# First loop of a two-layer transformer kernel: queries and keys projected once, their split parts placed by on-chip transfers

## The chip, the cores and the metric

The kernel runs on one core of a Trainium2 chip. The metric is the device time of one execution of the whole program in microseconds (us). The core has five engines that run their own instruction streams and wait for one another through semaphores: PE (TensorE, matmuls), DVE (VectorE), ACT (ScalarE), POOL (GpSimd) and SP (SyncE, which here only issues transfers, or DMAs).

## The reference, cut to what matters

The program is a layer of four blocks, twice over. The change touches the first block alone, whose attention part is this, for B = 16 batches of N = 256 rows of D = 128 numbers, in H = 16 heads of Dh = 8:

```python
q = (x @ Wq).reshape(B, N, H, Dh)
k = (x @ Wk).reshape(B, N, H, Dh)
scores = jnp.einsum('bqhd,bkhd->bhqk', q, k) * Dh ** (-0.5)
attn = jax.nn.softmax(scores, axis=-1)
std_out = jnp.einsum('bhqk,bkhd->bqhd', attn, v).reshape(B, N, D)
```

The same block has a second path (distances to 64 "splats", a small feed-forward net over them, a gate), an output projection and a layer norm. The two largest and smallest twentieths of the weights of a later feed-forward block are found by a search over the bits of a threshold, which runs beside the first loop: 32 rounds, each with a candidate threshold, a comparison of all weights with it, a count, and a decision.

## The kernel before, in words

`build` runs `loop_1`, `loop_2` and `phase_3` one after the other; only `loop_1` is touched. It takes the 16 batches as 128 pair steps, eight for a batch, each for one pair of heads. The list `stages` (L434 to L444) places every other piece of work at an offset in steps from its batch's first pair step, and each engine runs its own part of the list in the list's order (`run_in_order`, L213). So at pair step g the engine does `pair_step(g)`, then all stages that are due. In this text "odd 4" is pair step 4 of an odd-numbered batch, "even 0" pair step 0 of an even one.

**The heads' rows.** The scores need float32 accuracy from a matmul that reads rounded numbers (float32r). Each head has 32 partitions: three blocks of eight rows with the query (or key) in split form, then two rows for the row maximum, which are 1 on the key's side. With q = qh + ql and k = kh + kl (rounded part and rest) the three blocks multiply qh·kh, qh·kl and ql·kh. Four heads lie in the 128 partitions of one group, so `qT` and `kT` have four groups. To get this layout the weights are padded and repeated three times (`wq_pad`, `wk_pad`, L846 to L851), so that a batch needs four projections of two groups each: q0, k0, q1, k1 at offsets -8, -6, -4, -2 (`project_qk`, L475). ACT rounds each of them (`round_qk`, L740), DVE subtracts, by a per-partition factor 0 or -1 (`split_qk`, L905), and so writes the part that belongs to each row.

**The pair step.** PE computes the scores of a pair (L629) into the one buffer `ps_scores`, DVE takes the row maxima (L1021) and frees it. Eleven steps later (LAG) PE computes the same scores transposed with the maximum subtracted (L638) into the one buffer `ps_scoresT`, ACT takes the exponential (L812). On odd steps PE multiplies with the values (L651), and ACT reads the result (L820). The maxima of a batch go through DVE, PE (`turn_rows`, L585), ACT (L799) and four transfers of SP (`place_rows`, L1106) into two rows of each head of `qT`; PE waits for them at step 3 of the next batch.

**The four banks.** Everything else that PE writes goes through four PSUM banks. `PlannedRing.open` (L107) picks the bank whose planned release is the earliest and lets PE wait until it has been read.

**The search.** DVE makes a candidate (L950) in steps 1 and 5, after its decision on the round before; POOL compares the weights with it (four instructions, L1061); PE counts (`count`, L574) in step 4 and in step 0 of the next batch; DVE decides (L958 to L964) one step later. Each of these waits for the one before.

**SP's queue.** In order, in a batch's cycle: `place_rows` (offset 8, so step 0), `store` (offset 33, step 1), `load` of x and the context (offset -11, step 5, with the weight loads of the first three batches). SP runs ahead until a wait stops it. PE turns the loaded x (`project_x`, L472) in step 6, two batches ahead.

Of the kernel before, what the change touches and what calls it, by code (L numbers as in the profile page):

```python
# [28 lines left out]
P = 128  # L29
# [217 lines left out]
def loop_1(nc, A, K, x_mid):  # L247
    U = 16
    with ExitStack() as ctx:
        def sb(name, shape, dt=F32):  # L250
            return ctx.enter_context(nc.sbuf_tensor(name, shape, dt))
# [10 lines left out]
        wq = sb("wq_pad", [P, GROUPS, 4, 32])  # L262
        wk = sb("wk_pad", [P, GROUPS, 4, 32])
# [55 lines left out]
        rounded = two("qk_rounded", [P, 2 * N], F32R)  # L319
        qT = sets(3, "qT", [P, GROUPS, N], F32R)  # L320
        kT = sets(3, "kT", [P, GROUPS, N], F32R)
# [40 lines left out]
        wq_ready = sem("query_weights_ready")  # L362
        wk_ready = sem("key_weights_ready")
# [22 lines left out]
        rounded_ready = Counted(sem("rounded_ready"))  # L386
# [40 lines left out]
        for n in sizes:  # L427
# [4 lines left out]
        PIECE = NS // 2 // 4  # L432

# [3 lines left out]
            (-11, "load"), (33, "store"), (-8, "q0"), (-6, "k0"), (-4, "q1"), (-2, "k1"), (5, "gather"),  # L437
# [5 lines left out]
            (-8, "split_q0"), (-6, "split_k0"), (-4, "split_q1"), (-2, "split_k1"), (8, "turn_rows"),  # L443
# [5 lines left out]
        def _(pe):  # L449
# [25 lines left out]
            def project_qk(u, name, w, half):  # L475
                if name == "q" and half == 0:
                    ring.wait_read(pe, "xT", u)
                if u == 0 and half == 0:
                    pe.wait_ge(wq_ready if name == "q" else wk_ready, 1)
                ps = ring.open(pe, name, u, half, held=0.95)  # L480
                for g in range(2):
                    mm = pe.matmul(ps[:, g * N:(g + 1) * N], w[:, 2 * half + g, :, :].rearrange("p j d -> p (j d)"),
                                   xT[u][:], start=True, stop=True)
                mm.then_inc(ring.filled(name, u, half), 1)
# [141 lines left out]
            def scores(n, i, t):  # L626
                u, p = divmod(n, PAIRS)
                q, j = p // 2, 32 * (2 * (p % 2) + i)
                mm = pe.matmul(s_ps[:, i, t, :], qT[u][j:j + 3 * DH0, q, t * P:(t + 1) * P], kT[u][j:j + 3 * DH0, q, :],  # L629
                               start=True, stop=True)  # L630
                if t == NT - 1:
                    mm.then_inc(scores_full.sem, 1)

            def scores_T(n, i, kt):
# [3 lines left out]
                mm = pe.matmul(t_ps[:, i, kt, :], kT[u][j:j + rows_read, q, kt * P:(kt + 1) * P],  # L638
                               qT[u][j:j + rows_read, q, :], start=True, stop=True)
# [16 lines left out]
            def pair_step(g):  # L656
# [33 lines left out]
            steps = dict(project_x=project_x, q0=lambda u: project_qk(u, "q", wq, 0), k0=lambda u: project_qk(u, "k", wk, 0),  # L690
                         q1=lambda u: project_qk(u, "q", wq, 1), k1=lambda u: project_qk(u, "k", wk, 1), vg=project_vg,
# [11 lines left out]
        def _(act):  # L703
# [34 lines left out]
            order = [("q", 0), ("k", 0), ("q", 1), ("k", 1)]  # L738

            def round_qk(u, i):  # L740
                name, half = order[i]
                n = 4 * u + i
                if n == 1:
                    act.wait_ge(split_ready, 1)
                ps = ring.wait(act, name, u, half)
                if n >= 2:
                    before = order[(n - 2) % 4]
                    ring.wait_read(act, before[0], (n - 2) // 4, before[1])
                if name == "q":
                    act.activation(rounded[n][:], ps[:], ACT.Copy).then_inc(rounded_ready.sem, 1)  # L750
                else:
                    act.activation(rounded[n][:], ps[:], ACT.Identity, bias=pad_ones[:]).then_inc(rounded_ready.sem, 1)
# [69 lines left out]
            steps = dict(project_x=project_x, q0=lambda u: round_qk(u, 0), k0=lambda u: round_qk(u, 1),  # L822
                         q1=lambda u: round_qk(u, 2), k1=lambda u: round_qk(u, 3), vg=read_vg, influence0=influence0,
# [7 lines left out]
        def _(dve):  # L831
            setup = Chain(dve, dve_setup)
            setup.add(dve.memset(wk[:], 0.0))
            setup.add(dve.memset(wq[:], 0.0))
# [10 lines left out]
            for i in range(3):  # L845
                ins = dve.tensor_scalar(wq[:, :, :, DH0 * i:DH0 * (i + 1)], wq_raw[:].rearrange(heads, g=GROUPS, j=4),  # L846
                                        DH0 ** -0.5, None, ALU.mult)
            ins.then_inc(wq_ready, 1)
            for i in range(3):
                ins = dve.tensor_copy(wk[:, :, :, DH0 * i:DH0 * (i + 1)], wk_raw[:].rearrange(heads, g=GROUPS, j=4))  # L850
            ins.then_inc(wk_ready, 1)  # L851
# [51 lines left out]
            order = [("q", qT, 0), ("k", kT, 0), ("q", qT, 1), ("k", kT, 1)]  # L903

            def split_qk(u, i):  # L905
                name, dst, half = order[i]
                ps = ring.bank(name, u, half)
# [131 lines left out]
        def _(pool):  # L1039
# [5 lines left out]
            for i in range(3):  # L1045
                setup.add(pool.memset(v[i][:], 0.0))
# [2313 lines left out]
```

## Time and profile before

| | us |
|---|---|
| median of three runs | 1932.77 (1927.73 to 1934.17) |
| span of the profiled execution | 1930.1 |
| first loop within it | 0 to about 479 |
| PE busy in the whole span | 1723.1 (89%) |
| DVE, ACT, POOL busy | 1374.7, 1189.4, 1037.7 |

The profiled execution is 2.7 us below the median, inside the spread of the three runs. Busy shares are over all three phases; the chain that ended last, in the page's fourth part, lies in the last phase and says nothing of the first loop. For a change in the first loop one has to read that loop's own stretches and its order of time.

### The profile page before, as it was taken

The numbers are of one execution on the slowest core, as the hardware profiler recorded it, in microseconds if no ns is written. First come the engines' busy times: TensorE is split into PE (matmuls) and PEld (weight loads), VectorE is DVE, ScalarE is ACT, GpSimd is POOL, SyncE is SP. The second block draws the span as 40 slices with busy tenths as digits, with TensorE's granted clock in tenths as the row PEclk, the third lists the DMA queues.
The fourth block names the chain that finished last, engine by engine and source line by source line (L and its number), as shares of the span: only waits on it lengthen the run. The fifth ranks groups of instructions, "written<-read, shape, count | busy, mean of one in ns | idle before, by whom it ended". The sixth has DMA issues, their size and how long they took to land. (4 is left out here: it accounts for less than half of the span.)

```text
span 1930.1 us, 43925 instructions
## 1 busy us (share of the span) xinstructions
PE 1723.1 (89%) x15676; PEld 1312.7 (68%) x15676; DVE 1374.7 (71%) x4606; ACT 1189.4 (62%) x2858; POOL 1037.7 (54%) x1590
## 2 busy tenths in 40 slices
PE   7999999988899999999999999999879999589930
PEld 5666666656777777777777777776656667479930
DVE  6788888873767788888888888897657876611127
ACT  3566666642688777778778777776315776244412
POOL 3566676663245565655666565666421442175375
PEclk8999999999999999999999999999988999689975
DMA  2000000000200000000000000000000000345322
GB/s 56 9 13 15 15 16 15 12 5 27 75 1 2 1 2 7 8 7 8 7 8 7 6 3 7 6 4 6 6 27 15 27 21 16 99 70 75 60 64 83
DMA packets 57824, 44.03 MB, mean 23 GB/s; under 512 B 13952, under 2 KB 50186, under 8 KB 57482
## 3 DMA queue, kind: packets, MB, share of 16 engines
q1 hardware_dynamic: 52330, 30.11, 5.4%
q0 software_dynamic: 4608, 9.45, 3.3%
q8 instruction: 129, 2.11, 0.4%
q10 hardware_dynamic: 672, 1.67, 0.2%
q14 instruction: 85, 0.70, 0.1%
HBM read 26.52 MB, written 13.63 MB: 21 GB/s over the span
## 5 line engine op out<-in xcount | busy, mean ns | idle before, releaser
L2281 POOL TENSOR_SCALAR probs<-probs,rsums 128x128 f32<-128x128 f32 (+1 forms) x512 | 208.7, 426 | 307.6 <-DVE rsums L2178 306.7
L1061 POOL TENSOR_SCALAR at_least<-magnitudes,candidates 128x512 bf16<-128x512 f32 x128 | 198.2, 1564 | 151.3 <-DVE candidates L950 151.3
L2162 DVE CUSTOM_DVE_ANT_0 probs<-dist,pq,nmin 128x128 f32<-128x128 f32 (+1 forms) x512 | 181.2, 409 | 76.0 <-PE pq L1622 75.6
L1902 ACT ACTIVATE probs<-probs,low 128x130 f32<-128x130 f32 (+1 forms) x512 | 227.7, 460 | 6.3 <-DVE low L2162 6.2
L1021 DVE TENSOR_REDUCE negmax<-ps_scores 128x4 f32<-128x1024 f32 x128 | 156.2, 1221 | 53.6 <-PE ps_scores L629 51.9
L812 ACT ACTIVATE pT<-ps_scoresT 128x1024 f32<-128x1024 f32 x128 | 131.1, 1024 | 61.8 <-PE ps_scoresT L638 55.2
L2172 DVE COPY pT<-pq 128x384 f32<-128x384 f32 x256 | 129.8, 547 | 4.1 <-PE pq L1637 4.1
L1815 ACT ACTIVATE qn<-pq 128x512 f32<-128x512 f32 x128 | 77.2, 603 | 81.4 <-PE pq L1479 79.8
L1622 PE MATMUL pq<-k1T,q1T 64*128 64x128 f32 (+1 forms) x1024 | 119.3, 351 | 0.4 <-ACT k1T L1830 0.3
L3302 POOL DMA_INDIRECT m_x<-token_rows,m_idx_put x80 | 75.8, 947 | 80.7 <-DVE m_idx_put L3232 33.3
L3254 DVE COPY m_y<-pm 128x256 f32<-128x256 f32 x40 | 17.0, 424 | 140.6 <-PE pm L3140 140.6
L2087 DVE TENSOR_REDUCE ss<-sq 128x8 f32<-128x512 f32 x128 | 84.3, 675 | 30.9 <-ACT sq L1818 29.9
L1902 ACT ACTIVATION_READ_ACCUMULATOR probs<-probs,low 128x1 f32 x512 | 104.3, 204 | 0.0
L2898 DVE TENSOR_REDUCE cnegmax<-pc_scores 128x8 f32<-128x1024 f32 x64 | 78.2, 1222 | 25.8 <-PE pc_scores L2568 25.7
L1637 PE MATMUL pq<-ident,probs 128*128 128x128 f32 x512 | 91.4, 274 | 0.0
L2935 POOL TENSOR_SCALAR crstd<-cmv 128x4 f32<-128x4 f32 x16 | 3.7, 233 | 158.0 <-DVE cmv L2809 158.0
L2760 ACT ACTIVATE cpT<-pc_scoresT 128x1024 f32<-128x1024 f32 x64 | 65.5, 1024 | 33.7 <-PE pc_scoresT L2577 33.6
L1657 PE MATMUL pr_heads<-pT,v 128*64 128x256 f32 x512 | 83.5, 405 | 0.0
L1622 PEld LDWEIGHTS pq<-k1T,q1T 64*128 64x128 f32 x1024 | 67.5, 187 | 23.1 <-issue 22.2
L1671 PE MATMUL pr_out<-wo,o1T 128*128 128x128 f32 x512 | 77.9, 275 | 3.7 <-DVE l_r L2019 3.7
L1634 PE MATMUL pq<-ident,probs 128*128 128x128 f32 x256 | 77.3, 302 | 3.5 <-POOL probs L2281 3.4
L3140 PEld LDWEIGHTS pm<-m_w,m_hid 128*128 128x128 f32 x640 | 77.6, 192 | 2.0
(543 smaller groups left out, 5293.4 us busy)
## 6 DMA issues: line engine op xcount, KB each, us to landing
expert_answers<-m_y SPq DMA_DIRECT2D x40, 128.0 KB, 2.0
m_w<-in_L_ffn_moe_w_dram SPq DMA_DIRECT2D x16, 256.0 KB, 5.9
x<-in_x_dram SPq DMA_DIRECT2D x16, 128.0 KB, 2.2
x_mid<-x SPq DMA_DIRECT2D x16, 128.0 KB, 1.8
y<-x_mid SPq DMA_DIRECT2D x16, 128.0 KB, 2.2
x_mid<-y SPq DMA_DIRECT2D x16, 128.0 KB, 1.8
cx<-x_mid SPq DMA_DIRECT2D x8, 256.0 KB, 3.0
token_rows<-c_hn SPq DMA_DIRECT2D x8, 256.0 KB, 2.0
```

The costliest lines, as they stand in the source:

```text
L812: act.activation(pT[:, n % NPT].rearrange("p i k n -> p (i k n)"), t_ps[:].rearrange("p i k n -> p (i k n)"), ACT.Exp).then_inc(pT_ready.s ...
L1021: dve.tensor_reduce(negmax[u][:, :, j:j + 2, q].rearrange("p t j -> p j t"), s_ps[:], AX.X, ALU.max, negate=True).then_inc(negmax_ready.se ...
L1061: pool.tensor_scalar(at_least[:, a, :], mags[:, 512 * (a // 2):512 * (a // 2) + 512], cf[:, a:a + 1], None, ALU.is_ge).then_inc(mask_ready ...
L1622: mm = pe.matmul(ps[i][:, t * P:t * P + w], q1T[u][64 * i:64 * i + 64, p, t * P:(t + 1) * P], k1T[u][64 * i:64 * i + 64, p, 0:w], start=Tr ...
L1637: mm = pe.transpose(ps[:, (kt + 1) * P:(kt + 2) * P], probs[:, a + 1, first_key + kt * P:first_key + (kt + 1) * P], ident[:])
L1657: pe.matmul(tgt[:, 0:N], v1[u][:, 0, h * DH1:(h + 1) * DH1], pT[:, b, 0:2].rearrange("k t q -> k (t q)"), start=True, stop=False, skip_gro ...
L1902: ins = act.activation(probs[:, a, keys_nulls(i, w)], probs[:, a, keys_nulls(i, w)], ACT.Exp, bias=low[:, a, i:i + 1], scale=-1.0, accum_o ...
L2087: dve.tensor_reduce(ss[:, a, t, 8 * j:8 * j + 8], sq[:, j, :].rearrange("p (h d) -> p h d", d=DH1), AX.X, ALU.add).then_inc(ss_ready.sem, 1)
L2162: ins = dve.tensor_tensor_reduce(probs[:, a + t, keys(i, w)], dist[:, (1 - t) * P:N], ps[:, t * P:t * P + w], slopes[h], nmin[u][:, t, h:h ...
L2172: dve.tensor_copy(pT[:, (2 * m + i) % 4].rearrange("k t q -> k (t q)"), ps[:, 0:3 * P])\
L2281: ins = pool.tensor_scalar(probs[:, a + t, keys(i, w)], probs[:, a + t, keys(i, w)], rsums[:, a + t, i:i + 1], 1.0, ALU.mult, ALU.mult)
L2898: dve.tensor_reduce(negmax[u][:, :, j:j + 2, q].rearrange("p t j -> p j t"), s_ps[:], AX.X, ALU.max, negate=True).then_inc(negmax_ready.se ...
```

## The change

Queries and keys are projected once, without padding: the weight columns are reordered so that partition 32·j + 4·d + g holds number d of the head in place j of group g. One stage `qk` at offset -9 takes the place of q0, k0, q1, k1: two 256-column matmuls for a batch in place of eight. ACT rounds both into `parts` blocks 0 and 3 (one instruction in place of four), DVE writes the rests into blocks 1 and 2 (one in place of four) and signals after a wait. SP then places them: `place_qk` at offset -6 issues twelve DMAs a batch, each from 32 partitions of `parts` (two blocks of 256 numbers, 64 KB in all) into the eight rows of one part of one head place, in all four groups, of a joined `qkT`. The buffer has three sets as before, so from the fourth batch on the transfers wait until the last transposed scores of three batches earlier have been read. The ones on the key's side are written once by POOL at the start. Two clears of the padded weights on DVE go.

```diff
-            (-11, "load"), (33, "store"), (-8, "q0"), (-6, "k0"), (-4, "q1"), (-2, "k1"), (5, "gather"),
+            (-11, "load"), (33, "store"), (-9, "qk"), (5, "gather"),
...
-            (-8, "split_q0"), (-6, "split_k0"), (-4, "split_q1"), (-2, "split_k1"), (8, "turn_rows"),
+            (-9, "rest_qk"), (8, "turn_rows"), (-6, "place_qk"),
...
+            def project_qk(u):
+                ring.wait_read(pe, "xT", u)
+                if u == 0:
+                    pe.wait_ge(wqk_ready, 1)
+                ps = ring.open(pe, "qk", u, held=0.95)
+                for i, w in enumerate((wq, wk)):
+                    mm = pe.matmul(ps[:, i * N:(i + 1) * N], w[:].rearrange("p j d g -> p (j d g)"), xT[u][:],
+                                   start=True, stop=True)
+                mm.then_inc(ring.filled("qk", u), 1)
...
-                    if p % 4 == 0:
-                        ring.wait_read(pe, "k", u, p // 4)
+                    if p == 0:
+                        pe.wait_ge(*qk_placed[u % 2].at(PLACED * (u // 2 + 1)))
...
+            def round_qk(u):
+                ps = ring.wait(act, "qk", u)
+                if u >= 2:
+                    act.wait_ge(*qk_placed[u % 2].at(PLACED * (u // 2)))
+                act.activation(parts[u][:, 0:4:3, :], ps[:].rearrange("p (i n) -> p i n", i=2), ACT.Copy)\
+                    .then_inc(rounded_ready.sem, 1)
...
-            setup.add(dve.memset(wk[:], 0.0))
-            setup.add(dve.memset(wq[:], 0.0))
...
+            def rest_qk(u):
+                ps = ring.bank("qk", u)
+                dve.wait_ge(*rounded_ready.at(u + 1))
+                dve.tensor_tensor(parts[u][:, 1:3, :], ps[:].rearrange("p (i n) -> p i n", i=2),
+                                  parts[u][:, 0:4:3, :].bitcast(F32), ALU.subtract).then_inc(rest_ready.sem, 1)
+                dve.wait_ge(*rest_ready.at(u + 1))
+                dve.sem_inc(ring.read("qk", u), 1)
...
+            for i in range(3):
+                ins = pool.memset(qkT[i][:, :, 1, :].bitcast(F32), 1.0)
+            ins.then_inc(pool_keys, 1)
...
+                def place_qk(u):
+                    if u == 0:
+                        sp_eng.wait_ge(pool_keys, 1)
+                    sp_eng.wait_ge(*rest_ready.at(u + 1))
+                    if u >= 3:
+                        sp_eng.wait_ge(*pT_ready.at(PAIRS * (u - 2)))
+                    for j in range(4):
+                        for part, blocks in enumerate((slice(0, 4, 3), slice(0, 3, 2), slice(1, 4, 2))):
+                            rows_to = slice(32 * j + DH0 * part, 32 * j + DH0 * (part + 1))
+                            sp_eng.dma_start(qkT[u][rows_to].bitcast(F32),
+                                             parts[u][32 * j:32 * j + 32, blocks, :].bitcast(F32))\
+                                .then_inc(qk_placed[u % 2].sem, 16)
```

## Rows read from the trace of the kernel before

**Rows 1.** Windows, 50 us of the loop: us; busy (instructions) of PE, PEld, DVE, ACT, POOL; clock; DMA; GB/s

```profile
200.00:250.00 50.00, 46.89 (x584) 32.75 (x582) 42.04 (x107) 31.68 (x62) 33.75 (x31) 1.00 0.05 15
```

**Rows 2.** Groups by line, 150 to 350 us: line engine op out<-in shapes xcount | busy, mean ns | idle

```profile
L482 PE MATMUL ps<-xT,wk_pad 128*128 128x256 f32 x64 | 18.1, 405 | 0.0
L750 ACT ACTIVATE qk_rounded<-ps 128x512 fp32r<-128x512 f32 x16 | 9.6, 597 | 0.0
L909 DVE SCALAR_TENSOR_TENSOR qT<-qk_rounded,split_rows,ps 128x512 fp32r<-128x512 f32 x16 | 11.9, 742 | 1.4 <-DVE mixedT L999 1.3
```

**Rows 3.** Timeline of PE, one odd and one even batch: start us, us, engine line [idle before]

```profile
202.43 0.64 PE L585 MATMUL ps<-ident_r,max_rows 128*8 128x128 f32 x8 [1.09 <-DVEq L1002]
203.00 0.39 PE L629 MATMUL ps_scores<-kT,qT 24*128 24x256 f32 x2
207.85 0.39 PE L629 MATMUL ps_scores<-kT,qT 24*128 24x256 f32 x2 [0.76 <-DMA qT<-max_rowsT]
212.64 1.11 PE L574 MATMUL ps<-at_least,ones_bf 128*128 128x64 bf16 x32
213.69 0.38 PE L629 MATMUL ps_scores<-kT,qT 24*128 24x256 f32 x2
216.61 0.39 PE L629 MATMUL ps_scores<-kT,qT 24*128 24x256 f32 x2
218.53 0.39 PE L629 MATMUL ps_scores<-kT,qT 24*128 24x256 f32 x2
219.80 0.46 PE L622 MATMUL ps<-xw_folded,cT 128*128 128x128 f32 x2 [0.76 <-ACT xsqT L727]
222.53 0.39 PE L629 MATMUL ps_scores<-kT,qT 24*128 24x256 f32 x2
225.69 0.39 PE L629 MATMUL ps_scores<-kT,qT 24*128 24x256 f32 x2
238.65 0.39 PE L629 MATMUL ps_scores<-kT,qT 24*128 24x256 f32 x2
242.73 0.38 PE L629 MATMUL ps_scores<-kT,qT 24*128 24x256 f32 x2
245.77 0.39 PE L629 MATMUL ps_scores<-kT,qT 24*128 24x256 f32 x2
254.19 0.39 PE L629 MATMUL ps_scores<-kT,qT 24*128 24x256 f32 x2
```

**Rows 4.** Timeline of DVE and of POOL in the same odd batch

```profile
206.37 6.22 POOL L1061 TENSOR_SCALAR at_least<-magnitudes,candidates 128x512 bf16<-128x512 f32 x4 [5.71 <-DVE candidates L950]
...
217.18 1.23 DVE L1021 TENSOR_REDUCE negmax<-ps_scores 128x4 f32<-128x1024 f32 x1
```

**Rows 5.** Timeline of PE in batch 15, odd 1 to odd 5, with no projections left

```profile
411.93 0.38 PE L629 MATMUL ps_scores<-kT,qT 24*128 24x256 f32 x2
421.54 1.11 PE L574 MATMUL ps<-at_least,ones_bf 128*128 128x64 bf16 x32 [1.09 <-POOL at_least L1061]
422.93 0.38 PE L629 MATMUL ps_scores<-kT,qT 24*128 24x256 f32 x2
```

**Rows 6.** The page's list of DMA issues: xcount, KB each, us to landing

```profile
x<-in_x_dram SPq DMA_DIRECT2D x16, 128.0 KB, 2.2
```

**Rows 7.** Line L2994, four 16 KB placements in a later phase: ns min/median/max

```profile
L2994 SPq DMA_DIRECT2D cqT<-c_rowsT x32: 596/611/752, 1456.1 to 1620.6; - x32
```

**Rows 8.** Timeline at the loop's start, DVE and PE

```profile
8.92 0.75 DVE L909 SCALAR_TENSOR_TENSOR qT<-qk_rounded,split_rows,ps 128x512 fp32r<-128x512 f32 x1 [1.77 <-ACT qk_rounded L750]
...
15.99 0.50 PE L629 MATMUL ps_scores<-kT,qT 24*128 24x256 f32 x4
...
23.63 2.07 PE L482 MATMUL ps<-xT,wk_pad 128*128 128x256 f32 x4
...
41.65 1.76 PE L574 MATMUL ps<-at_least,ones_bf 128*128 128x64 bf16 x32 [1.42 <-POOL at_least L1061]
```

**Rows 9.** Window of 5 us in batch 15, columns as in rows 1

```profile
415.00:420.00 5.00, 3.65 (x48) 2.10 (x48) 4.71 (x13) 2.57 (x4) 4.70 (x4) 1.00 0.09 28
```

More of the change, by code:

```diff
@@ L318, in loop_1 @@
         xsqT = two("xsqT", [P, N])
-        rounded = two("qk_rounded", [P, 2 * N], F32R)
-        qT = sets(3, "qT", [P, GROUPS, N], F32R)
-        kT = sets(3, "kT", [P, GROUPS, N], F32R)
+        parts = two("qk_parts", [P, 4, N], F32R)
+        qkT = sets(3, "qkT", [P, GROUPS, 2, N], F32R)
         v = sets(3, "v", [P, NT, H0, 32])
@@ L385, in loop_1 @@
         pT_ready = Counted(sem("probsT_ready"))
-        rounded_ready = Counted(sem("rounded_ready"))
+        rounded_ready = Counted(sem("qk_rounded_ready"))
+        rest_ready = Counted(sem("qk_rest_ready"))
+        qk_placed = [Counted(sem(f"qk{i}_placed")) for i in range(2)]
         on_ready = Counted(sem("o_normal_ready"))
@@ L473, in project_x @@
                 pe.transpose(ps[:, 256:256 + S_CTX], c[u][:], ident[0:S_CTX, 0:S_CTX]).then_inc(ring.filled("xT", u), 1)
[L475 to L484, printed above, removed]
+            def project_qk(u):
[7 more added lines that the diff above has]
+                mm.then_inc(ring.filled("qk", u), 1)
             def project_vg(u):
@@ L637, in scores_T @@
                 rows_read = 3 * DH0 + 2
[L638 to L639 removed]
+                mm = pe.matmul(t_ps[:, i, kt, :], qkT[u][j:j + rows_read, q, 1, kt * P:(kt + 1) * P],
+                               qkT[u][j:j + rows_read, q, 0, :], start=True, stop=True)
                 if kt == 1:
@@ L688, in values_step @@
                     values((g - LAG - 2) // 2)
-            steps = dict(project_x=project_x, q0=lambda u: project_qk(u, "q", wq, 0), k0=lambda u: project_qk(u, "k", wk, 0),
-                         q1=lambda u: project_qk(u, "q", wq, 1), k1=lambda u: project_qk(u, "k", wk, 1), vg=project_vg,
+            steps = dict(project_x=project_x, qk=project_qk, vg=project_vg,
                          distances=distances, splats=splats, turn_out=turn_out, fold_cross=fold_cross, influence_tm=influence_tm, gather=gather,
@@ L736, in fold_cross @@
                 act.activation(w_x[:], ps[:, 0:D], ACT.Copy).then_inc(w_x_ready, 1)
[L738 to L752, printed above, removed]
+            def round_qk(u):
[4 more added lines that the diff above has]
+                    .then_inc(rounded_ready.sem, 1)
             def read_vg(u):
@@ L820, in values_step @@
                     act.activation(oT[u][:, q, :], ps[:, 0:N], ACT.Copy).then_inc(ring.read("o", u, q), 1)
-            steps = dict(project_x=project_x, q0=lambda u: round_qk(u, 0), k0=lambda u: round_qk(u, 1),
-                         q1=lambda u: round_qk(u, 2), k1=lambda u: round_qk(u, 3), vg=read_vg, influence0=influence0,
+            steps = dict(project_x=project_x, qk=round_qk, vg=read_vg, influence0=influence0,
                          influence_tm=influence_tm, gather=gather, encode=encode, decode=decode, turn_rows=max_rows,
@@ L844, in _ @@
             dve.wait_ge(qk_loaded, 16 * len(qk_loads))
[L845 to L851, printed above, removed]
+            dve.tensor_scalar(wq[:].rearrange("k j d g -> k g j d"), wq_raw[:].rearrange(heads, g=GROUPS, j=4),
+                              DH0 ** -0.5, None, ALU.mult)
+            dve.tensor_copy(wk[:].rearrange("k j d g -> k g j d"), wk_raw[:].rearrange(heads, g=GROUPS, j=4))\
+                .then_inc(wqk_ready, 1)
             dve.wait_ge(pool_ready, 1)
@@ L901, in link @@
                 chain(ins)
[L903 to L907, printed above, removed]
-                dve.wait_ge(*rounded_ready.at(4 * u + i + 1))
-                dve.scalar_tensor_tensor(dst[u][:, 2 * half:2 * half + 2, :].rearrange("p g n -> p (g n)"),
-                                         rounded[4 * u + i][:].bitcast(F32), split[:, i % 2:i % 2 + 1], ps[:],
-                                         ALU.mult, ALU.add).then_inc(ring.read(name, u, half), 1)
+            def rest_qk(u):
[5 more added lines that the diff above has]
+                dve.sem_inc(ring.read("qk", u), 1)
             def fold_cross(u):
@@ L1118, in pair_step @@
                     pass
-                steps = dict(load=load, turn_rows=place_rows, store=store)
+                steps = dict(load=load, turn_rows=place_rows, place_qk=place_qk, store=store)
                 run_in_order(stages, PAIRS, U, steps, pair_step)
```

19 lines of the change are left out of this document (9 added, 10 removed).

## The prediction

> **What bounds the kernel now.** The page comes first, but its shares average three phases; the windows of the first loop's steady stretch tell more [rows 1]. PE is busy 46.9 of 50 us, DVE 42.0, POOL 33.8, ACT 31.7, at full clock. So PE looks like the bound, and the change takes six of eight projection matmuls a batch from it. Before crediting that I read the timeline of PE against DVE and POOL for two batches [rows 3, 4], because this loop consists of short steps with single buffers, where a lighter engine only meets the next wait. The pattern repeats every two batches: odd 1 starts at 203.00 and again at 254.19, so two batches take 51.19 us, and the windows from 150 to 370 us show the same.
>
> Three waits lie close behind PE. First, **the pair step has a floor**: DVE starts its reduction 0.57 us after the scores (217.18 against odd 6 at 216.61) and takes 1.23 [rows 3, 4]; PE's next scores follow about 0.05 later, so no step is shorter than 1.86 us. Second, **the search**: odd 1 starts at 203.00, POOL compares from 206.37, when DVE's candidate is there, for 6.22 us, to 212.59, and PE counts at 212.64 [rows 3, 4]. That count follows `q1` without idle time, yet it couldn't have started earlier. Batch 15 proves it: there, with no projections left, PE stands 1.09 us idle before the count, and odd 1 to odd 5 still takes 422.93 - 411.93 = 11.00 us, against 10.69 in the steady odd batch [rows 3, 5]. Third, **the maxima**: `turn_rows` waits 1.09 us in odd 0 for a bank that DVE frees at L1002, and odd 3 waits 0.76 us for the placed rows [rows 3].
>
> **What is removed and added.** On PE a projection of two groups is four instructions whose union is 18.1 / 16 = 1.13 us [rows 2], overlapping its neighbours by some 0.1: 1.0 us of PE's time. Four such become one: 3.0 us a batch less, in steps 0, 2, 4, 6 (1.0 each), and 1.0 more in step 7. DVE loses four L909 of 0.742 and gains one subtraction over as many numbers, at the same price: 2.2 us less a batch. ACT loses two instructions of 0.597 and two of the key's kind, about as long, and gains one of 0.6: 1.8 us or more less. Neither sets the pace by its sum; they matter where they stand in front of a wait.
>
> **The sum by segments of the two-batch pattern** [rows 3, 4]; step lengths are differences of L629 starts, and parts of a step not in the rows are read between them in the same timeline:
> - Odd 1 to odd 4, 213.69 - 203.00 = 10.69 us. The search gives 3.37 (start of POOL's work) + 6.22 + 0.05 + 1.05 (count) = 10.69 at the least. Steps 2 and 4 get 1.0 lighter each, and both turn into idle time before the count. Gain 0.0.
> - Odd 5 to even 0, 225.69 - 213.69 = 12.00 us. Odd 6 is at 218.53 - 216.61 = 1.92 already and can fall to 1.86. Odd 7 (222.53 - 218.53 = 4.00) gets the new projection, +1.0. It loses the 0.76 of idle time before L622: that is a bank wait on `xT`'s bank, and I worked through the ring's choices with the new list of openings; L622 gets another, long free bank. But in the new choice the values of odd 7 get the bank of `encode`, which ACT reads only after its exponential, the new rounding (0.6) and the two `encode` reads (0.64): free about 3.95 us into the step, where PE would be ready at 3.15. So +0.75. Even 0 (3.16) has its scores and count done after 1.5 us and waits for DVE's maxima at 2.3, then 0.7: 3.0. Segment: 12.00 - 0.06 + 1.0 - 0.76 + 0.75 - 0.16 = 12.77, a loss of 0.77.
> - Even 1 to even 4, 238.65 - 225.69 = 12.96 us. PE alone would fall by 2.0, but the search gives 3.37 + 6.22 + 0.05 + 1.03, and `transform2` 1.02 behind the count: 11.69. Gain 1.27.
> - Even 5 to odd 0, 254.19 - 238.65 = 15.54 us. Even 6 (245.77 - 242.73 = 3.04) falls to the floor, -1.18. Even 7 gets +1.0, and about 0.2 of waiting for `xT`'s copies, since step 6 is shorter. Odd 0 gains only 0.3: the first half of `turn_rows` gets another bank, the second still the one freed at L1002. Gain 0.3.
>
> Together 0.8 us in two batches, out of the 6 that PE sheds. The projections of batches 1 to 15 run in steps 0 to 119, seven such patterns after batch 0: **-6 us**.
>
> **Placing.** SP can start `place_qk` only when the exponential of step 2 is done, 4.2 us after odd 1 (5.3 after even 1). No row shows such a transfer. The nearest is L2994, also from more partitions to fewer, 0.611 us of SP each [rows 7]; the floor is x's or its like, 0.36 to 0.4, the top some 1 us. With 0.61: 7.3 us for twelve. `load` stands behind them in SP's queue: it issues x and c by 12.0 us after odd 1, they land 2.2 us after issue [rows 6], at about 14.1, and `project_x` in odd 6 wants them at 10.69 + 2.92 + 0.44 = 14.05. In even batches 15.2 against 16.2. So this is hidden with nothing to spare in odd batches beyond the 0.8 us by which odd 6 lies under its floor. The data are wanted only at step 0, six microseconds and more after they land. The bytes, 768 KB a batch, are bounded by nothing from below, if they flow while SP issues, and from above by taking x's 2.2 us for 128 KB as all transfer, 13.2 us. I take the first, as the context's 32 KB take 2.2 us too, so that most of it seems fixed; the issue of 7.3 us sets the pace. Cost 0, range 0 to 20 us over the loop.
>
> The Trainium skill speaks against this change here: "DMA: Bandwidth & Descriptors", section "Why a DMA increments its semaphore by 16 and not by 1", says that a DMA is spread over the largest number of engines up to 16 that divides both outermost sizes, so 32 rows into 8 would use eight. By it the upper bound doubles to about 26 us, an estimate, and so does the loop's loss under it; no row of before shows it.
>
> **The start.** Here work is added to the path. Batch 0's rests are written at 9.7 us (as L909 now, 8.92 + 0.75) [rows 8]. SP then issues twelve transfers to 17.0, and only then `load` of batch 1, formerly done at 5 us; PE's stream has `project_x` and `qk` of batch 1 ahead of the first scores. x lands at about 19.7, turned and copied 21.6, projected at low clock (2.07 us for four instructions [rows 8]) 23.7. So the first scores come at 23.7 in place of 15.99, +7.7. But the first steps wait for the search too: the first candidate moves from 21.2 to about 28.9, the first count from 30.7 (where it had 2.9 us of slack after POOL's 27.75) to 35.2, the second from 41.65 to about 45.5, and with a shorter `turn_rows` wait behind it odd 1 of batch 1 comes 3 us late: **+3 us**, between 0 and +8.
>
> Sum: 1930.1 - 6 + 3 = 1927.1 for the profiled execution; with its 2.7 us below the median, 1929.8, so **1930 us**.
>
> **The rivals.** (a) *PE was the bound after all.* Then 15 batches gain 3.0 each: 1932.8 - 45 + 3 = 1891. Its milder form keeps the search and the floor but drops the bank wait in odd 7 and the loss at the start: -1.6 × 7 = -11, so 1921. Rows 1 speak for it, rows 5 against it. 0.15 together. (b) *SP's queue becomes the bound* (slower). From 0.66 us per placement on, `project_x` waits in odd 6, from about 0.70 in even 6. At 0.8 us: (0.8 - 0.66) × 12 = 1.7 and (0.8 - 0.70) × 12 = 1.2 us, 2.9 in two batches, × 7 = +20: 1950; bandwidth-limited transfers (13.2 us) give +9 in two batches and 1990. The skill's eight engines raise this. 0.2. (c) *The clock.* PE falls from 47 to about 42 busy us in 50, and where the granted clock falls to half, work of 5 us takes 10. Five drops, one more in three batches, at some 2.5 us each (the stretches at 115 and 135 us cost about that): +12, 1942. Against it: in batch 15 PE is busy 3.65 of 5 us at clock 1.00 [rows 9]. "TensorE: Matmul & The Clock Gate" of the Trainium skill, section "HAM oscillation — how this bites in real kernels", warns that repeated waits throw the clock back; that row disagrees for waits as short as these. 0.08. (d) *It doesn't do what it says*, for instance compiled to the same order of waits: 1933. 0.02.
>
> **Chances and range.** The forecast has 0.55, with an own spread of ±8 us (1922 to 1938), as each step's ±0.5 us in a pattern is ±3.5 and the start ±4. Range 1912 to 1950: it takes in (a)'s mild form, (c), and half of (b). A measurement of this kernel can tell about 0.3% (5.8 us) from no change, so faster is below 1927. That is 0.17 of the forecast's 0.55 and all of (a): 0.32. Slower, above 1938.6, is 0.05 of the forecast, (b) and most of (c): 0.29. Same: 0.39.
>
> **What would show it.** Right: idle time before L574 behind POOL in odd 4 and even 4, steps 6 at 1.86 us, two batches in about 50.4 us, a first L629 near 24 us. Wrong: two batches near 46 (a); PE idle before L472 on a DMA, with issues over 0.66 us (b); more windows of the loop at a clock below 1.00 (c). If odd 7 stays near 4.2 us, the ring step was wrong. It all falls if POOL's comparisons get shorter than 6.2 us, as then the search frees PE.

## The result, and the profile after

| | before | after |
|---|---|---|
| median, us | 1933.47 (1927.73 to 1941.17) | 2033.4 (2026.26 to 2043.35) |
| span of the profiled execution | 1930.1 | 2028.5 |
| start of odd 0 of batch 1 | 38.7 | 54.1 |
| start of odd 0 of batch 15 | 407.7 | 500.8 |
| start of the 53 fillers that close the first loop | 469.8 | 565.9 |

A filler is an idle matmul on the identity that `hold_clock` (L228 to L233) issues. The ratio is 1.0515, 95% interval 1.047 to 1.0561: the change costs 5%, about 100 us. The forecast was 1930 us, the range ended at 1950; both were wrong. Of the 98.4 us between the two profiled spans 93.1 are there at odd 0 of batch 15 and 96.2 at the end of the first loop. They split into 15.4 us at the start and 77.6 us in the fourteen batches between (446.7 us against 369.1; "the stretch" below).

A window of 50 us of the kernel after, with the columns of rows 1:

```profile
200.00:250.00 50.00, 44.98 (x427) 29.66 (x427) 26.01 (x67) 21.01 (x43) 21.86 (x22) 0.70 0.15 24
```

Against rows 1 the other engines do about two thirds of their work in the same time, and PE is still busy 45.0 of 50 us. It isn't busy with more: the granted clock is 0.70 in place of 1.00. So there are two things to find, who waits, and why the clock is down. The waits of the kernel after, 0 to 600 us (us in total, times, longest), name the first:

```profile
PE ps L474 <- DMA c<-in_ctx_dram: 56.9, 14, 14.7
PEld ps L474 <- DMA c<-in_ctx_dram: 55.7, 13, 15.6
```

That is `project_x`, waiting in nearly every batch for the context that `load` brings (PEld loads PE's weights, so its row is the same wait seen a second time). SP's and PE's timelines around even 6 show why, and what follows:

```profile
218.61 9.72 SPq L1099 DMA_DIRECT2D qkT<-qk_parts  x12
228.38 0.45 SPq L1076 DMA_DIRECT2D x<-in_x_dram  x1
228.87 0.53 SPq L1077 DMA_DIRECT2D c<-in_ctx_dram  x1
...
230.24 0.38 PE L630 MATMUL ps_scores<-qkT 24*128 24x256 f32 x2
...
233.40 0.44 PE L474 MATMUL ps<-ident,x 128*128 128x128 f32 x2 [2.66 <-DMA c<-in_ctx_dram]
...
235.10 0.58 PE L630 MATMUL ps_scores<-qkT 24*128 24x256 f32 x2
...
242.70 1.94 PE L652 MATMUL ps<-pT,v 128*32 128x256 f32 x16
...
244.56 0.58 PE L630 MATMUL ps_scores<-qkT 24*128 24x256 f32 x2
```

The twelve placements hold SP for 9.72 us; the context is issued at 228.87 and used at 233.40, 4.5 us later. PE stands still for 2.66 us, and even 7 (235.10 to 244.56) then takes 9.46 us. Its values L652 take 1.94 us for sixteen matmuls, 1.07 at full clock. Windows of 5 us over the same steps, last columns clock, DMA share and GB/s:

```profile
225.00:230.00 5.00, 5.00 (x76) 4.21 (x72) 3.73 (x12) 1.83 (x4) 1.07 (x2) 1.00 0.60 78
230.00:235.00 5.00, 2.34 (x23) 1.40 (x15) 2.23 (x5) 2.24 (x7) 5.00 (x4) 0.87 0.28 38
235.00:240.00 5.00, 5.00 (x23) 3.16 (x22) 2.48 (x6) 1.79 (x5) 1.36 (x3) 0.50 0.00 0
240.00:245.00 5.00, 5.00 (x34) 2.50 (x32) 0.69 (x1) 1.23 (x4) 1.86 (x3) 0.50 0.01 3
```

So a wait of under 3 us is followed by two windows at half clock (1.2 GHz), in which PE is busy without a break and does little. In windows of 1 us the clock is at 0.50 from 234 to 247.

The rows that answer to rows 6 and 7 (the page's list of DMA issues, then line L1099 with min/median/max in ns, then the landing times of the context's load, L1077):

```profile
x<-in_x_dram SPq DMA_DIRECT2D x16, 128.0 KB, 3.6
```

```profile
L1099 SPq DMA_DIRECT2D qkT<-qk_parts x192: 673/686/1674, 9.9 to 490.1; - x192
```

```profile
DMA to landing us min/median/max: 2.5/5.4/6.6
```

And the start, which answers to rows 8 (timelines of SP and PE):

```profile
9.86 8.83 SPq L1099 DMA_DIRECT2D qkT<-qk_parts  x12
18.73 0.45 SPq L1076 DMA_DIRECT2D x<-in_x_dram  x1
...
25.91 0.69 PE L474 MATMUL ps<-ident,x 128*128 128x128 f32 x2 [14.72 <-DMA c<-in_ctx_dram]
...
29.92 0.79 PE L630 MATMUL ps_scores<-qkT 24*128 24x256 f32 x4
```

### The profile page after: what moved, and what is told of

Same layout as the page of the kernel before. It is cut to its first block and busy times, and to the rows that moved or that the text cites. A ratio compares the mean times of both kernels' runs of the same rounds, so it can differ in the third digit from the quotient of the medians.

```text
span 2028.5 us, 43614 instructions
## 1 busy us (share of the span) xinstructions
PE 1761.5 (87%) x15484; PEld 1322.3 (65%) x15484; DVE 1342.0 (66%) x4552; ACT 1161.8 (57%) x2810; POOL 1040.6 (51%) x1593
## 5 line engine op out<-in xcount | busy, mean ns | idle before, releaser
L2084 DVE TENSOR_REDUCE ss<-sq 128x8 f32<-128x512 f32 x128 | 84.3, 675 | 30.9 <-ACT sq L1815 29.9
L1634 PE MATMUL pq<-ident,probs 128*128 128x128 f32 x512 | 91.3, 274 | 0.0
L630 PE MATMUL ps_scores<-qkT 24*128 24x256 f32 x512 | 74.5, 374 | 17.3 <-DMA qkT<-max_rowsT 8.9
L652 PE MATMUL ps<-pT,v 128*32 128x256 f32 x1024 | 84.4, 457 | 2.1 <-ACT enc L776 1.9
L630 PEld LDWEIGHTS ps_scores<-qkT 24*128 24x128 f32 x512 | 45.3, 217 | 57.9 <-issue 35.1
```

The costliest lines, as they stand in the source:

```text
L630: mm = pe.matmul(s_ps[:, i, t, :], qkT[u][j:j + 3 * DH0, q, 0, t * P:(t + 1) * P], qkT[u][j:j + 3 * DH0, q, 1, :], start=True, stop=True)
L652: mm = pe.matmul(ps[32 * j:32 * j + 32, 0:N], v[u][:, kt, 4 * q + j, :], pT[:, (2 * m + j // 2) % NPT, j % 2, kt, :], start=(kt == 0), sto ...
L1634: mm = pe.transpose(ps[:, (kt + 1) * P:(kt + 2) * P], probs[:, a + 1, first_key + kt * P:first_key + (kt + 1) * P], ident[:])
L2084: dve.tensor_reduce(ss[:, a, t, 8 * j:8 * j + 8], sq[:, j, :].rearrange("p (h d) -> p h d", d=DH1), AX.X, ALU.add).then_inc(ss_ready.sem, 1)
```

## The experiments

Two quantities beside the ratio are read from each trace: the stretch (odd 0 of batch 1 to odd 0 of batch 15, by the starts of the scores), and **the low clock** in it, the sum over windows of 5 us of 2 · (1 - clock) · 5 us, that is the time spent at half clock. Before has 14 us of it, after 190. The median of the kernel before differed between chips, from 1931 to 1975 us, so each ratio is against the kernel before on the same chip. The other columns come from one trace each, on several chips. By these traces and by the ratios the kernels differ from before by the same amounts within 9 us, so a difference of a few microseconds between two stretches is not resolved.

| kernel | ratio (95%) | first scores | odd 0 of b. 1 | stretch | low clock |
|---|---|---|---|---|---|
| before | 1 | 16.0 | 38.7 | 369.1 | 14 |
| after | 1.0515 (1.047 to 1.0561) | 29.9 | 54.1 | 446.7 | 190 |
| e1 loads first | 1.0232 (1.0202 to 1.0262) | 30.5 | 52.0 | 396.8 | 122 |
| e2 few bytes | 1.0277 (1.0206 to 1.0348) | 29.7 | 51.7 | 405.3 | 146 |
| e3 before + 8 rows | 1.0421 (1.0381 to 1.046) | 28.7 | 59.9 | 429.4 | 96 |
| e4 before + 32 rows | 1.0135 (1.0083 to 1.0188) | 23.0 | 48.5 | 379.0 | 27 |
| e5 hold clock | 1.0406 (1.037 to 1.0442) | 31.7 | 53.9 | 435.0 | 123 |
| e6 no projection | 1.004 (1.0016 to 1.0063) | 15.3 | 40.9 | 381.5 | 100 |
| e7 e1 + fillers in scores | 1.0423 (1.0389 to 1.0458) | 30.3 | 51.6 | 436.7 | 101 |
| e8 e7, weights later | 1.041 (1.0378 to 1.0442) | 26.8 | 51.5 | 436.4 | 81 |
| e9 e1 + fillers | 1.0142 (1.0106 to 1.0179) | 30.4 | 51.9 | 377.8 | 14 |
| e10 e9, weights later | 1.0104 (1.0067 to 1.014) | 27.0 | 51.8 | 379.3 | 20 |
| e11 e6 + fillers | 0.9995 (0.9963 to 1.0026) | 15.3 | 40.9 | 365.3 | 10 |
| e12 e11, half the fillers | 1.0014 (0.9981 to 1.0046) | 16.0 | 38.5 | 366.7 | 31 |

### e1: the loads ahead of the placements

```diff
-            (-11, "load"), (33, "store"), (-9, "qk"), (5, "gather"),
+            (-14, "load"), (33, "store"), (-9, "qk"), (5, "gather"),
```

> The changed kernel with one number changed: SP's `load` is due three steps earlier, so x and the context of the batch after next are issued ahead of the twelve placements, not behind them. Theory: the loss is x landing late behind the placements in SP's queue, and the low clock that PE's idle time there brings. Then the wait before project_x (112.6 us in 27 waits over PE, half of it a weight load's and half a matmul's) goes, step 6 falls from 5 to 6.5 us to about 1.9, step 7 from 7.6 to 9.5 us to about 5, and the total falls by some 80 us, to 1930 to 1955. Rival 1, the transfers themselves slow the engines (SBUF or queue contention): the waits go and steps 3 and 7 stay long, 1990 or more. Rival 2, the clock falls because PE has less to do, whatever it waits for: step 6 is short but clock stays at 0.66 to 0.8 in half of the windows, total about 1980.

Measured: the context lands 2.1 us after its issue, PE no longer waits for it, and the stretch falls by 49.9 us to 396.8. Of the 77.6 us lost in the stretch about two thirds go with the order of SP's queue. The expectation of 80 us in all was too high: 1.0232 is about 1978 against 1933, the outcome of rival 2. What remains isn't a wait for data: 122 us of low clock, with no load late. Batches 8 and 9 are among the quickest, at 52.4 us together, and in both step 3 takes 4.9 us (3.35 before) at a lowered clock.

### e2: the same twelve transfers, one thirty-second of the bytes

```diff
-                            sp_eng.dma_start(qkT[u][rows_to].bitcast(F32),
-                                             parts[u][32 * j:32 * j + 32, blocks, :].bitcast(F32))\
+                            sp_eng.dma_start(qkT[u][rows_to, :, :, 0:8].bitcast(F32),
+                                             parts[u][32 * j:32 * j + 32, blocks, 0:8].bitcast(F32))\
```

> The changed kernel, whose twelve placements move 8 of 256 numbers of each piece: the same 64 pieces each, one 32nd of the bytes; most of the scores' rows are left at 1, so the scores are others. Load still stands behind them. Theory bytes: 64 KB in pieces of 1 KB are what delays x's landing (5.4 us for the context against 2.2); then it lands 2.2 us after issue, SP's 0.686 us per placement stays, and the total falls to 1935 to 1975. Rival, number of pieces or the issue: landing stays near 5 us and the total near 2030.

POOL fills the rows that the transfers no longer reach with ones, once at the start. Measured: the issue stays at 686 ns, so its price is not the bytes', but the context lands after 2.4 us. PE's waits for it, from 30 to 460 us:

```profile
PE ps L474 <- DMA c<-in_ctx_dram: 7.2, 6, 2.9
```

Behind the start after has 37.7 us of them (56.9 less the first two, 4.4 and 14.7). The stretch falls by 41.4 us. The ratio, 1.0277, lies above the range that was expected, as the low clock stays at 146 us. So of the 49.9 us that e1 gets back, most hangs on the bytes still in flight in front of x and the context, and less on SP's time.

### e3 and e4: the kernel before with twelve extra transfers

Both add a stage `place_extra` to the kernel before, at the place of `place_qk`. It moves a constant into a buffer that nobody reads, 64 KB a transfer as in the change. Between the two only the receiving side differs: 8 partitions, or the same 32 that the rows come from.

```diff
 e3
+                            sp_eng.dma_start(extra_dst[32 * j + 8 * part:32 * j + 8 * part + 8], extra_src[32 * j:32 * j + 32, 0:4:3, :])
 e4
+                            sp_eng.dma_start(extra_dst[32 * j:32 * j + 32, part], extra_src[32 * j:32 * j + 32, 0:4:3, :])
```

> The kernel before, all its projections kept, with twelve placements a batch added at the same place of SP's queue, of the same shape (32 partitions into 8, 64 KB), from a constant tile into one that nobody reads. Theory: the placements cost their price without any of the rest of the change: total 1933 + 85 to 1933 + 110, about 2025, with PE idle before project_x on the load. Rival: the loss comes from the new order of work on PE, ACT and DVE (steps 0 to 7, banks): then this run stays below 1960.

> As e3_before_plus_8rows, with the same number of extra transfers, bytes and source, but into 32 partitions of the tile in place of 8. Theory from the page's rule of the dividing number of engines: 16 engines share each in place of 8, the transfers drain in half the time, the context lands 2.2 to 3 us after its issue in place of 5 or more, and the wait before project_x, 111 us over both halves of PE in e3_before_plus_8rows, falls to 70 or less (SP's issue of 0.7 us each stays). Rival, the rate is one of SBUF to SBUF transfers whatever their shape: same waits, same total as e3.

Measured, first e3 and then e4, each with the transfers' line and, from 30 to 460 us, PE's wait for the context:

```profile
L1121 SPq DMA_DIRECT2D extra_dst<-extra_src x192: 673/686/1884, 11.7 to 477.3; - x192
...
PE ps L476 <- DMA c<-in_ctx_dram: 37.1, 12, 4.9
```

```profile
L1121 SPq DMA_DIRECT2D extra_dst<-extra_src x192: 588/597/1714, 11.5 to 413.7; - x192
...
PE ps L476 <- DMA c<-in_ctx_dram: 8.2, 7, 1.8
```

The queue's share of the sixteen engines' time, 0 to 460 us, again e3 and then e4:

```profile
q1 hardware_dynamic: 28616, 18.22, 27.0%
```

```profile
q1 hardware_dynamic: 31607, 19.37, 17.2%
```

Into 8 partitions the context lands 5.7 us after its issue, into 32 partitions 2.3. For fewer bytes the first takes more of the engines' time. The ratios are 1.0421 (81 us, just under the 85 to 110 expected) and 1.0135. So the shape of the transfer, its issue and its landing together, carries about 2.9% of this kernel's time, with PE's work unchanged, and a lighter PE isn't needed for the waits. e4 also shows that even 0.597 us each isn't free here: odd 6 takes 2.7 to 3.5 us from batch 3 to batch 13, 1.92 before.

### e5: fillers in front of the wait for the load

```diff
                 ps = ring.open(pe, "xT", u, held=0.7)
+                if u >= 3:
+                    hold_clock(pe, ps[:, 0:N], ident, 24)
+                pe.wait_ge(*x_loaded[u % SETS].at(32 * (u // SETS + 1)))
```

> The changed kernel with 24 small matmuls into the bank of xT before PE's wait for the load, from the fourth batch on, some 2.6 us of work in place of idle time. Theory: half of the loss is the low clock behind the wait. Then the waits stay nearly as long with the filler counted in, step 7 falls from 7.6 to 9.5 us to 4.5 to 5.5, and the total falls by 30 to 50 us, to 1985 to 2005. Rival, the clock falls for another reason: no change, 2030, or the filler's own 2 us a batch more.

Measured: PE has something to run while it would have stood still, and in most batches step 7 is back at 5.0 to 5.4 us (8.65 to 9.46 in batches 4, 6, 8, 10 and 12 of after). The stretch falls by only 11.7 us, as the fillers also run where the load is early, step 6 remains long, and the low clock, 123 us, now sits in other steps. So the slow step 7 is the clock's answer to the wait, but the wait isn't all that lowers the clock, and the 30 to 50 us that were expected did not come.

### e6: the kernel before without its projections

Left out from batch 3 on: the projections of queries and keys, their rounding and their splitting. The rest is unchanged.

```diff
                 if name == "q" and half == 0:
                     ring.wait_read(pe, "xT", u)
+                if u >= 3:
+                    return
```

> The kernel before without any projection, rounding and splitting after batch 2: later batches take the rows of batches 0 to 2 as queries and keys (left out: those batches' own projections). No placements, no queue: PE alone is 4 us a batch lighter, more than the change makes it. By my sum (search, pair-step floor, maxima bind next) batches 1 to 14, 369.1 us in the kernel before, get only some 15 to 25 us shorter. Rival, PE was the bound: 45 us or more shorter. Rival, a PE with less to do falls to the low clock: the stretch gets no shorter or longer than 369 us, with 100 us or more of it at the low clock, against 14 us in the kernel before.

Measured: ratio 1.004, and the stretch grows from 369.1 to 381.5 us, though 4 us of PE's work a batch is gone. No placement and no late load is in this kernel; what it shares with the change is less work on PE, and on ACT and DVE. The window that answers to rows 1, and three windows of 5 us from later on:

```profile
200.00:250.00 50.00, 43.31 (x538) 28.66 (x538) 36.37 (x94) 27.38 (x53) 32.58 (x29) 0.88 0.05 15
...
295.00:300.00 5.00, 5.00 (x49) 3.16 (x49) 2.13 (x10) 1.36 (x4) 2.81 (x2) 0.66 0.00 0
300.00:305.00 5.00, 3.94 (x26) 2.62 (x26) 4.20 (x9) 3.57 (x10) 3.38 (x3) 0.83 0.01 3
305.00:310.00 5.00, 5.00 (x37) 2.41 (x36) 0.73 (x4) 0.72 (x3) 2.51 (x4) 0.50 0.00 0
```

PE's timeline around them, with every idle time between 290 and 304 us:

```profile
291.75 1.11 PE L576 MATMUL ps<-at_least,ones_bf 128*128 128x64 bf16 x32 [0.40 <-POOL at_least L1067]
...
297.25 1.94 PE L653 MATMUL ps<-pT,v 128*32 128x256 f32 x16
...
301.26 0.38 PE L631 MATMUL ps_scores<-kT,qT 24*128 24x256 f32 x2 [0.19 <-DVE negmax L1027]
...
302.64 0.46 PE L624 MATMUL ps<-xw_folded,cT 128*128 128x128 f32 x2 [0.87 <-DVEq L1000]
```

In shorter windows the clock falls to 0.50 twice, at 296.5 and at 303.3 us. No single idle time is long (in the whole stretch the longest is 1.6 us), and ahead of the first fall the profile shows PE busy without a break for 4.7 us. So the traces show that the lighter kernel loses its clock, not by which of its pauses. Step 7 of this even batch takes 7.7 us against 4.3 before.

### e7 and e8: fillers put into the scores, and an earlier load

```diff
 e7: e1, and in pair_step
+                if straight and turned and g % 2 == 0 and g > 12:
+                    pe.wait_ge(*pT_ready.at(g - LAG))
+                    hold_clock(pe, t_ps[:, 0, 0, :], ident, 8)
 e8: e7, and the weight loads of loads 1 and 2 issued behind the placements of batch 0
```

> The changed kernel with loads ahead of the placements, as in the run e1_loads_first, plus eight small filler matmuls (about 0.9 us, the time of a removed projection) at the head of every even pair step, ahead of PE's wait for the maxima. Clock theory: the 122 us at low clock between odd 0 of batch 1 and of batch 15 shrink to below 50, and that stretch from 396.8 to 365 to 380 us, although PE has more to do; total at 1.00 to 1.012 of the kernel before. Rival, the new order of work holds the loop back: the filler adds its time, 400 us or more.

> As e7_loads_first_filler, and the weight loads that stood behind the load of batch 1 go behind the placements of batch 0. Theory of the start (a queue that holds 12 placements ahead of what the first scores need): first scores at 22 to 25 us in place of 30.5, total 4 to 7 us less than e7_loads_first_filler. Rival, the start is hidden by the search: no difference at batch 1.

Measured: a failure of the remedy. The fillers stand in front of the scores of even-numbered steps, behind the odd-numbered ones, in which PE has work without a gap, and lengthen these. The stretch becomes 436.7 us, 40 us worse than e1's, with 101 us of low clock. In it, too, the clock falls behind work without a gap: at 282.7 us, 9 us after PE's last idle time (0.32 us). What fillers do depends on where they stand. e8 brings the first scores from 30.3 to 26.8 us, but odd 0 of batch 1 from 51.6 only to 51.5. PE never waits for the search in between. Its matmuls run longer than in e7, four scores 0.79 us against 0.50 at step 5, as at half clock, though the profile's clock says 1.00 there for both.

### e9 and e10: fillers where the projections were

```diff
 e9: e1, with stages (-8, "fill0"), (-6, "fill1"), (-4, "fill2"), (-2, "fill3")
+            def fill(u, i):
+                if u < 1:
+                    return
+                ps = ring.open(pe, "fill", u, i, held=0.3)
+                hold_clock(pe, ps[:, 0:N], ident, 8).then_inc(ring.filled("fill", u, i), 1)
+                hold_clock(pe, ps[:, 0:N], ident, 1).then_inc(ring.read("fill", u, i), 1)
 e10: e9 with e8's order of the weight loads
```

> The changed kernel with loads ahead of the placements (e1_loads_first) and, at the very places where the four projections of a batch stood, nine small filler matmuls each, some 1.0 us, into a bank that PE itself frees. e7_loads_first_filler had its filler at the heads of even steps, that is behind the long odd steps. Clock theory: PE's busy share comes back to 93% or more, the low-clock time between odd 0 of batch 1 and of batch 15 falls from 122 us to below 40, and the stretch from 396.8 to 365 to 378 us, though PE does some 57 us more of work; total at 1.00 to 1.012 of the kernel before. Rival, PE does too much and the new order (qk in step 7) holds it: the stretch stays at 397 us or grows.

> As e9_loads_first_fill, with the weight loads behind the placements of batch 0. It is the best form of the change that the runs so far point to. Expected first scores at 26 to 27 us, odd 0 of batch 1 unchanged within 1 us (51 to 52), total within 3 us of e9_loads_first_fill. Rival, the start is a real loss of 4 us that this gets back.

Measured, the window of e9 that answers to rows 1 (e1 has clock 0.69 there):

```profile
200.00:250.00 50.00, 48.07 (x580) 33.52 (x582) 36.64 (x97) 27.72 (x55) 31.51 (x28) 0.97 0.24 41
```

Four blocks of nine idle matmuls a batch are added to PE, and the stretch gets 19.0 us shorter (396.8 to 377.8); the low clock falls from 122 to 14 us, the value of before. The only thing taken away is low clock, so in e1 it cost these 19 us at the least; the two ratios, each against its own chip, are 0.009 apart, 17 us. The result is still 1.0142 times before, e10 1.0104, which their intervals don't tell apart. e10 brings the first scores to 27.0 us and odd 0 of batch 1 only to 51.8, because PE then waits for the placements of batch 1:

```profile
51.77 0.79 PE L637 MATMUL ps_scores<-qkT 24*128 24x256 f32 x4 [3.48 <-DMA qkT<-qk_parts]
```

### e11 and e12: the same fillers without projections

Both leave out what e6 leaves out.

```diff
 e11: e6, with e9's four fill stages (held=0.95, from batch 3 on)
 e12: e11 without fill1 and fill2 for the odd batches (they run in steps 2 and 4 of even ones)
```

> e6_no_projection (left out: projections after batch 2) with the same fillers in the place of the projections left out. No placements here. Clock theory: low-clock time falls from 100 us to below 35 and the stretch from 381.5 to between 355 and 369 us, total below e6_no_projection by 15 to 25 us, at 0.985 to 1.00 of the kernel before. Rival, the low clock came from something else (chance, a hot chip): 100 us of low clock stay and the filler adds to the time.

> As e11_no_projection_fill (left out: projections after batch 2), but without the fillers of steps 2 and 4 of even batches, where PE has the transforms to do and the filler lengthens the step. It asks whether there is anything to gain once the projections cost nothing and the clock is kept. If filler is needed only where PE would wait, even 1 to even 4 falls from 12.94 to the 11.7 us that the search allows, the stretch from odd 0 of batch 1 to odd 0 of batch 15 from 365.3 to 355 to 360 us, low clock stays below 30 us, total 0.99 to 0.997 of the kernel before. Rival, those fillers kept the clock: low-clock time goes back above 50 us and the stretch is no shorter than 365 us.

Measured for e11, the window of rows 1 and one of those shown for e6:

```profile
200.00:250.00 50.00, 47.21 (x623) 33.75 (x620) 36.43 (x99) 27.51 (x55) 34.15 (x32) 1.00 0.06 15
...
305.00:310.00 5.00, 4.34 (x51) 2.70 (x49) 4.62 (x15) 3.62 (x8) 2.53 (x2) 1.00 0.11 33
```

With fillers in the projections' places the clock stays up and the stretch falls from 381.5 to 365.3 us, 3.8 us below the kernel before; the median is the same (0.9995). By the ratios the gain over e6 is 9 us, less than the 15 to 25 expected. In e12 the steps that follow those without fillers show the price: even 3 takes 4.7 to 6.05 us (3.35 before) at a lowered clock, so even 1 to even 4 takes 12.8 us and not the 11.7 that was expected, and even 6 3.6 (3.04). So with no projections at all, and the clock held by these two sets of fillers, this kernel gains nothing that can be measured. Fillers that hold the clock at a lower price were not found.

## Why the prediction was wrong, and where it was right

**The sum by segments was right, and hardly counted.** In steps that no low clock and no late load touches, the traces have these lengths. Odd 1 to odd 4 (batch 13 of after): 2.51 + 2.28 + 3.36 + 2.51 = 10.66 us, forecast 10.69. Even 1 to even 4 (batch 4 of after): 3.54 + 1.86 + 3.35 + 2.98 = 11.73, forecast 11.69. Odd 5 to even 0, in e1: 2.92 + 1.86 + 5.02 + 3.05 = 12.85, forecast 12.77. Even 5 to odd 0, in e1: 4.08 + 1.85 + 5.55 + 3.84 = 15.32, forecast about 15.2. Together 50.6 us for two batches, pieced from several; the forecast said 50.4. No two batches of after or e1 show all of them at once; the best pair is e1's 52.4. The floor of 1.86 us and the search are therefore as described, and so is the bank wait in odd 7, forecast at 0.75 (e1):

```profile
252.90 1.07 PE L652 MATMUL ps<-pT,v 128*32 128x256 f32 x16 [0.69 <-ACT enc L776]
```

Rival (a) is dead: in e6, with all the projections away, odd 1 to odd 4 still takes 10.66 us (batch 9) and even 1 to even 4 11.72 (batch 10). But after needs 446.7 / 7 = 63.8 us for two batches.

**"Cost 0, range 0 to 20 us" for the placing failed.** The mechanism was named, with its threshold, as rival (b): above 0.66 us each, `project_x` waits in step 6. What failed is the size taken from rows 7. The start of the work was right: SP begins 5.3 us after even 1 (213.34, by the steps' starts), as forecast. Then come two mis-sized terms. Twelve issues take 8.7 to 9.7 us and not 7.3, and the context lands 4.5 to 5.4 us after its issue and not 2.2. That is 1.4 to 2.4 and 2.3 to 3.2 us, against 1.0 us of slack in even batches and none in odd ones. The near row had the right kind of transfer (many partitions to few) but 16 KB and not 64, and the landing time was taken from a queue with nothing in front. By e2 the second term is the larger one. The price also left the forecast's range, because each wait is followed by a slow step 7: 9.46 us in even 7, against 5.55 in e1 where its clock is up. The order of the queue costs 49.9 us in all (e1), where rival (b) at its worst had about 60 (1990 against 1930) from the bandwidth alone; by its own thresholds, 7.9 and 8.4 us for twelve, it is 10 us in two batches and not 9, so 70.

The Trainium skill, "DMA: Bandwidth & Descriptors", section "Why a DMA increments its semaphore by 16 and not by 1", says that a DMA uses the largest number of engines up to 16 that divides both outermost sizes: eight for 32 rows into 8. The runs agree with it: e3 and e4 move the same bytes, and the context behind them lands after 5.7 and 2.3 us. They don't prove it, since e3's rows also end in a quarter as many partitions, and e4's rows stay in their own; no run tells these apart. The forecast should have given that rule more than its 0.2.

**Rival (c) was dismissed by a row that could not speak for it.** Rows 9 show batch 15 at clock 1.00 with PE busy 3.65 of 5 us, and from that followed "waits as short as these" do no harm, and 0.08. But the lines of that window hold something I had read past. PE's timeline of the kernel before:

```profile
416.73 0.50 PE L232 MATMUL ps_scoresT<-ident 128*128 128x256 bf16 x3 [1.34 <-DVE negmax L1021]
```

This is `hold_clock`, which `pair_step` calls with three fillers in the last two batches and the first 24 steps, and nowhere between. So the row shows short waits with fillers in them, and the loop has none. Batch 15 of after, with the same fillers, answers to rows 9 and agrees:

```profile
505.00:510.00 5.00, 3.66 (x45) 2.15 (x44) 4.14 (x10) 3.62 (x7) 1.68 (x2) 1.00 0.11 34
```

That the fillers are what keeps the clock there is not shown. e6 has the same three in batch 15 and loses its clock in it all the same:

```profile
425.00:430.00 5.00, 4.23 (x29) 2.70 (x31) 2.71 (x6) 2.31 (x4) 0.00 (x0) 0.66 0.02 5
```

So one quiet window at 1.00 could not speak against (c), with or without fillers. In the loop e6 shows what less work brings: 100 us of low clock in place of 14 and a longer loop, and e1 122 us. What (c) had wrong is the number of drops. It allowed for five, and e1 has over 100 us more low clock than before. Its 2.5 us for one was rather high: the two drops at 115 and 135 us make batches 3 and 4 of before 54.0 us together, 2.8 more than the 51.2 of a quiet pair. Removing the clock's part from e1 gives 19.0 us (e9), and the low clock also comes on top of the waits of (b). "TensorE: Matmul & The Clock Gate" of the Trainium skill, section "HAM oscillation — how this bites in real kernels", which I set aside, describes a loop in which PE waits several microseconds for a transfer again and again and finds itself at the low clock each time. The waits of after agree with it (2.66 us in even 6, then 0.50). The falls in e6 come with far shorter pauses, which that section does not describe.

**The start, +3, was 15.4 us.** The placements begin at 9.86 as forecast (9.7), but take 8.83 us (7.3), and x and the context of batch 1 are used at 25.91 and not 19.7: the landing again. The first scores come at 29.9 (23.7). Of this delay of 13.9 us nothing is hidden: odd 0 of batch 1 comes 15.4 later. That the search gives part of it back is not borne out. e8 and e10 win 3.5 and 3.4 us at the first scores and have lost them at batch 1, but to slow matmuls and to a wait for placements, not to the search.

**The account of the 93.1 us** at odd 0 of batch 15: start 15.4; loads behind the placements, with the low clock that their waits bring, 49.9 (after to e1); low clock from a lighter PE alone 19.0 (e1 to e9, net of what the fillers cost); rest 8.7 (e9 to before). The rest is not taken apart by a run. In it are the heavier step 7, the fillers themselves, and waits of the scores for placed rows (5.7 us in four waits from 60 to 460 us of e9). The first term rests on the trace of after, the second and third on runs.

## What to carry to other kernels

Before a transfer is put in front of a load in a queue, price the load's landing as well as the issues: bytes in flight in front of it count, and so does the shape of the transfers that carry them (the landing falls from 5.4 us to 2.4 with few bytes in e2, from 5.7 to 2.3 with another shape in e4). Taking work from the engine that looks like the bound is worth nothing if the next wait is close, and here it costs, because PE with less to do lost its clock (e6); take a filler into the sum, or leave the work in. And a row cited against a rival has to come from the same regime and from more than one window: look in it for fillers.

## What the runs showed of the hardware that was not expected

- Twelve transfers of 64 KB from 32 into 8 partitions cost SP 686 ns each and delay a small load behind them to 5.7 us; from 32 into 32 partitions they cost 597 ns and delay it to 2.3 (e3, e4). With a thirty-second of the bytes the issue still takes 686 ns (e2).
- A PE that is busy 43.3 of 50 us, without one long wait, had a mean clock of 0.88 (e6). Idle matmuls in the places of the projections brought it to 1.00 and the stretch got 16.2 us shorter (e11); the same kind of filler at the end of steps that PE fills anyway made the loop slower (e7).
- The clock also fell behind 4.7 us (e6) and 9 us (e7) in which the profile shows no idle time of PE. What brings it down there is open.
- The low clock outlasts its cause: behind 2.66 us of idle time in even 6, PE ran two windows of 5 us at 0.50 though it was busy in all of both (after).
